# Earlier head products, earlier divisions and a separate bias matmul in an eight-layer transformer stack

## The reference

```python
# L2 attention
att = einsum('bhqd,bhkd->bhqk', q, k) / scale          # 512 x 512, 16 heads, causal
y = einsum('bhqk,bhkd->bhqd', softmax(att), v)
# L3 feed-forward, its head attention
h = _rmsnorm(x, gamma1)
q = (h @ Wq + bq).reshape(b, t, H, HD)
kv = ((h @ Wdown + bdown) @ Wup + bup).reshape(b, t, H, 2 * HD)
k, v = jnp.split(kv, 2, axis=-1)
att = jax.nn.softmax(einsum('bthd,btgd->bthg', q, k) / sqrt(HD), axis=-1)   # 16 x 16 per token
out = einsum('bthg,btgd->bthd', att, v)
```

## Time and profile before

| | |
|---|---|
| median of 3 runs | 6042.43 us (6034.11 to 6050.51) |
| profiled execution, its own time | 6034.11 us |
| its span | 6032.4 us, mean granted TensorE clock 0.875 of full |
| busy share | PE 78%, PEld 45%, DVE 61%, POOL 36%, ACT 31% |
| first maximum to last division of L2 attention, first pair | 134.3 us |
| DMA over the span | 24 GB/s |

### The profile page before, as it was taken

How to read it: one execution, slowest core, us unless ns; L and a number is a source line. 1 busy time by engine, 2 the same in 40 slices (tenths; PEclk the granted TensorE clock), 3 DMA queues, 4 the chain that set the end, 5 groups by cost and what they waited for, 6 DMA issues and landing times. The chain is left out here.

```text
span 6032.4 us, 97232 instructions
## 1 busy us (share of the span) xinstructions
PE 4713.6 (78%) x37160; PEld 2735.5 (45%) x37160; DVE 3697.0 (61%) x11081; ACT 1851.2 (31%) x2829; POOL 2161.3 (36%) x2704
## 2 busy tenths in 40 slices
PE   5979797979797979595877868778687786877772
PEld 3444445444444444363443544535435444354442
DVE  3646464646464646364768567686686766857765
ACT  2333343334333334242323224132331322412320
POOL 1323232323232222444525236153361443614525
PEclk9989898989898989797888888888888888888886
DMA  4000000000000000372000000000000000000000
GB/s 146 6 18 6 18 6 18 6 18 6 18 6 18 6 18 6 112 232 74 4 15 13 8 20 4 15 14 6 18 6 12 18 5 17 8 9 20 3 15 5
DMA packets 141914, 146.71 MB, mean 24 GB/s; under 512 B 31256, under 2 KB 126042, under 8 KB 141042
## 3 DMA queue, kind: packets, MB, share of 16 engines
q1 hardware_dynamic: 114274, 93.48, 5.3%
q0 software_dynamic: 18432, 37.79, 2.2%
q10 hardware_dynamic: 8736, 8.91, 0.5%
HBM read 69.64 MB, written 62.59 MB: 22 GB/s over the span
## 5 line engine op out<-in xcount | busy, mean ns | idle before, releaser
L792 DVE CUSTOM_DVE_ANT_0 twin<-twin,w_mask_row 128x512 f32<-128x512 f32 (+3 forms) x2048 | 951.0, 521 | 329.7 <-PE twin L1761 328.3
L1761 PE MATMUL twin<-arena 32*128 32x128 f32 (+3 forms) x4096 | 799.4, 517 | 39.6 <-DMA arena<-hres 16.8
L1779 PE MATMUL twin<-arena 32*128 32x128 f32 (+3 forms) x4096 | 784.2, 499 | 35.3 <-DVE arena L792 33.9
L1707 PE MATMUL twin<-w_ident_b 128*128 128x512 bf16 x1536 | 454.9, 450 | 383.7 <-DVE mv L752 157.9
L1435 ACT ACTIVATE arena<-twin 128x768 f32<-128x768 f32 (+1 forms) x544 | 479.3, 881 | 691.6 <-PE twin L1790 387.5
L1779 PEld LDWEIGHTS twin<-arena 32*128 32x128 f32 x4096 | 342.8, 195 | 471.7 <-issue 283.3
L695 POOL TENSOR_SCALAR ve<-mv 128x4 f32<-128x4 f32 x128 | 27.7, 216 | 1467.8 <-DVE mv L752 1467.2
L321 POOL DMA_INDIRECT got<-sorted_y,back x288 | 281.1, 976 | 539.6 <-ACT ring L1641 289.0
L1707 PEld LDWEIGHTS twin<-w_ident_b 128*128 128x128 bf16 x1536 | 157.7, 112 | 651.5 <-DVE mv L752 180.6
L313 POOL DMA_INDIRECT sorted_x<-got,w_mo_first_slots x288 | 282.4, 981 | 467.5 <-DVE ring L866 302.2
L1761 PEld LDWEIGHTS twin<-arena 32*128 32x128 f32 x4096 | 353.6, 204 | 196.8 <-issue 109.2
(11 more groups left out here) (440 smaller groups left out, 10008.1 us busy)
## 6 DMA issues: line engine op xcount, KB each, us to landing
sorted_y<-arena SPq DMA_DIRECT2D x96, 256.0 KB, 2.8
sorted_x<-zeros ACTq DMA_DIRECT2D x2, 4096.0 KB, 19.9
a<-sorted_x SPq DMA_DIRECT2D x64, 128.0 KB
b<-sorted_x SPq DMA_DIRECT2D x64, 128.0 KB, 2.5
hres<-sorted_x SPq DMA_DIRECT2D x64, 128.0 KB
sorted_x<-got,w_mo_first_slots POOLq DMA_INDIRECT x288
got<-sorted_y,back POOLq DMA_INDIRECT x288
x_out<-w_l_w SPq DMA_DIRECT2D x18, 256.0 KB, 2.3
```

Of the source, the lines that this page charges most:

```text
L792: last = dve.tensor_tensor_reduce(s[:, e, at:at + w], s[:, e, at:at + w], W["mask_row"][:, T - w:T], -1.0, 3e38, ALU.add, ALU.min, into)
L1707: pe.matmul(into, ident_b, ident_b.unsqueeze(1).broadcast_to([P, NT, P]), start=True, stop=True, skip_group_check=True)
L1761: last = pe.matmul(s[:, e, at:at + w], queries[r, P * i:P * (i + 1)], keys[r, 0:w], start=(at == 0), stop=True, skip_group_check=True)
L1779: last = pe.matmul(s[:, e, at:at + w], keys[r, P * m:P * (m + 1)], queries[r, P * m:T], start=(at == 0), stop=(tag == "l2"), skip_group_ch ...
```

## The change

It has four parts, all in the second loop.

- The products run two ahead: four of them stand before the first mask instead of two, and six quartets instead of seven carry two each. TAKE_STEP moves the reductions with them: the first four products are reduced from (-2, 3) to (0, 0), and the last two in quartet 6 instead of 7. `head_maxima`, `head_sums` and `head_outputs` on VectorE move from quartets 2, 3, 4, 5, 6 and 8 to 0, 1, 3, 4, 5 and 7, and `head_exponents` from (2, 3) and (5, 0) to (0, 3) and (4, 0).
- In every quartet of L2 attention `spread_sums` and `invert` move from step 3 to step 2, and `divide` from step 5 to step 3.
- The bias of the up-projection in `l3_front` is no longer a 65th row of ones in the down-projection's output. The down-projection gives 64 rows, the up-projection multiplies 64 rows, and a second matmul per token tile adds the bias: a row of ones, 1 x 128, by the bias, 1 x 256.
- The bias is a weight of its own, loaded once at the start.

```diff
@@ gpsimd, l2_masks and the layer loop @@
-                                        product(2 + 2 * c)
+                                        product(4 + 2 * c)
                                 if c < HEAD_QUARTETS:
-                                    product(3 + 2 * c)
+                                    product(5 + 2 * c)
...
-                                for m in range(2):
+                                for m in range(4):
                                     product(m)
                                 l2_masks()
@@ vector, twin_attention @@
-                                    if u == (2 if tag == "l1" else 5):
+                                    if u == (2 if tag == "l1" else 3):
                                         divide(c - 1)
@@ vector, l2_attention, beside @@
-                                if (c, u) == (2, 1):
+                                if (c, u) == (0, 1):
                                     head_maxima(0)
+                                if (c, u) == (1, 1):
+                                    head_sums(0)
                                 if (c, u) == (3, 1):
-                                    head_sums(0)
+                                    head_maxima(1)
                                 if (c, u) == (4, 1):
-                                    head_maxima(1)
+                                    head_sums(1)
                                 if (c, u) == (5, 1):
-                                    head_sums(1)
-                                if (c, u) == (6, 1):
                                     head_outputs(0)
-                                if (c, u) == (8, 1):
+                                if (c, u) == (7, 1):
                                     head_outputs(1)
@@ scalar, twin_attention and l2_attention @@
-                                    if tag == "l2" and u == 3:
+                                    if tag == "l2" and u == 2:
                                         invert(c - 1)
...
-                                if (c, u) == (2, 3):
+                                if (c, u) == (0, 3):
                                     head_exponents(0)
-                                if (c, u) == (5, 0):
+                                if (c, u) == (4, 0):
                                     head_exponents(1)
@@ tensor, twin_attention @@
-                                    elif u == 3:
+                                    elif u == 2:
                                         spread_sums(c - 1)
@@ tensor and scalar, l3_front @@
-                                pe.matmul(pb(q, 0)[0:65], W["l3f_wd"], F[q][:, PAD:], start=True,
+                                pe.matmul(pb(q, 0)[0:64], W["l3f_wd"], F[q][:, PAD:], start=True,
                                           stop=True).then_inc(sg["f_down_mm"], 1)
...
                                     o = pb3(q, 2 + t // 2, 2)[:, t % 2]
-                                    pe.matmul(o, ht_dt[q][0:65, t * P:(t + 1) * P], W["l3f_wup"], start=True, stop=True,
+                                    pe.matmul(o, ht_dt[q][0:64, t * P:(t + 1) * P], W["l3f_wup"], start=True, stop=False,
+                                              skip_group_check=True)
+                                    pe.matmul(o, W["ones"][0:1, :], W["l3f_bup"], start=False, stop=True,
                                               skip_group_check=True).then_inc(sg["f_kv_mm"], 1)
...
-                                act.activation(ht_dt[q][0:65], pb(q, 0)[0:65], ACT.Identity,
-                                               bias=W["l3f_bd"][0:65, 0:1]).then_inc(sg["f_dt"], 1)
+                                act.activation(ht_dt[q][0:64], pb(q, 0)[0:64], ACT.Identity,
+                                               bias=W["l3f_bd"][0:64, 0:1]).then_inc(sg["f_dt"], 1)
@@ tables @@
-HEAD_QUARTETS = 7
-TAKE_STEP = {(-1, 1): (0, 0), (-1, 2): (0, 1), (-1, 4): (1, 0), (0, 0): (1, 1)}
+HEAD_QUARTETS = 6
+TAKE_STEP = {(-2, 3): (0, 0), (-2, 4): (0, 1), (-1, 0): (1, 0), (-1, 1): (1, 1), (-1, 2): (2, 0), (-1, 3): (2, 1),
+             (-1, 5): (3, 0), (0, 0): (3, 1)}
...
-    TAKE_STEP[c_ + 1, 0], TAKE_STEP[c_ + 1, 2] = (2 + 2 * c_, 0), (2 + 2 * c_, 1)
+    TAKE_STEP[c_ + 1, 0], TAKE_STEP[c_ + 1, 2] = (4 + 2 * c_, 0), (4 + 2 * c_, 1)
@@ weights @@
+    a["l3f_wup"] = g["L3_ffn_Wup"].reshape(64, H, 2, DH).transpose(0, 2, 1, 3).reshape(64, 2 * D)
+    a["l3f_bup"] = g["L3_ffn_bup"].reshape(H, 2, DH).transpose(1, 0, 2).reshape(1, 2 * D)
```

More of the change, by code:

```diff
@@ L2373 @@
 BUSY = 6
-HEAD_QUARTETS = 7
-TAKE_STEP = {(-1, 1): (0, 0), (-1, 2): (0, 1), (-1, 4): (1, 0), (0, 0): (1, 1)}
+HEAD_QUARTETS = 6
+TAKE_STEP = {(-2, 3): (0, 0), (-2, 4): (0, 1), (-1, 0): (1, 0), (-1, 1): (1, 1), (-1, 2): (2, 0), (-1, 3): (2, 1),
+             (-1, 5): (3, 0), (0, 0): (3, 1)}
 for c_ in range(HEAD_QUARTETS):
-    TAKE_STEP[c_ + 1, 0], TAKE_STEP[c_ + 1, 2] = (2 + 2 * c_, 0), (2 + 2 * c_, 1)
-    TAKE_STEP[c_ + 1, 4], TAKE_STEP[c_ + 1, 5] = (3 + 2 * c_, 0), (3 + 2 * c_, 1)
+    TAKE_STEP[c_ + 1, 0], TAKE_STEP[c_ + 1, 2] = (4 + 2 * c_, 0), (4 + 2 * c_, 1)
+    TAKE_STEP[c_ + 1, 4], TAKE_STEP[c_ + 1, 5] = (5 + 2 * c_, 0), (5 + 2 * c_, 1)
 STATE_BANK = ((4, 5, 4), (6, 7, 5))
```

5 lines of the change are left out of this document (1 added, 4 removed).

## The result

The changed kernel takes 6239.39 us, the median of 4 runs (6223.85 to 6252.54), against 6038.95 (4 runs, 6034.11 to 6050.51): 1.0328 times as long, 95% interval 1.0302 to 1.0355. It is slower, as forecast, but by 200 us where the prediction had 74 to 79, and outside its range. The profiled execution took 6226.76 us, its span 6225.1 at a mean granted clock of 0.850 of full (before 0.875).

The account below looks back on a forecast made before the run. VectorE's list bounds L2 attention up to the shift of (5, 1); later TensorE waits for masks behind GpSimd's products. Attention +4.7 and bias +5.0 us, eight times, make 78, plus 0.5 once: 79, forecast 6116 us, range 6062 to 6150.

Parts of the forecast that it names:

- The bias matmul: End of the loop body: four more matmuls a sequence, 3.6 us, plus 1.4 for changes of shape, +5.0 us a body.
- Its bound of 8: Upper bound of the bias term: 8 us a body, at twice the passes' time.
- Spread sums a step earlier: L2 attention, quartets 1 to 5: about 0.5 us of new VectorE idle in each, +2.5 us a body.
- its bound of 5: Upper bound of the spread term: 5 us, if a half clock makes the spread take twice as long.
- The earlier division gives nothing back: L2 attention: dividing sooner gains nothing, since VectorE's total counts in that stretch, not its order.
- The subtraction: `head_maxima` at (0, 1): its subtraction meets a GpSimd product and takes the dearer earlier time, +1.1 us a body.
- `head_outputs`: The second head step moved to where a GpSimd product runs, at (5, 1): +0.5 us a body.
- The first rival: GpSimd's product holds the subtraction 2 us more, `head_outputs` 1 to 1.5: +3 us a body, 6140 us; chance 0.13.
- Reductions: VectorE up to the shift of (5, 1): more reductions +4.5, `head_outputs` +0.6, `head_sums` filling idle -1.5; sum +3.6 us.
- The tail: Quartets 6 and 7 lose their products, mask waits and half clock: 4.1 us gained, less spread delays, net -3 us.
- The rival of the low clock: Attention's third window has the low clock each time: +3.7 us a body, 30 in all, 6146 us; chance 0.07.

Follow-up runs that it names:

- e14: The changed kernel with VectorE's shift ahead of the head steps in step (c, 1); 1.0195 of before.
- e4: The kernel before with the bias part alone, its bias matmul having 64 rows (63 of zeros) instead of one; 1.0057 of before.
- e2: The kernel before with only spread_sums, invert and divide at their new steps; 1.0069 of before.
- e10: The kernel before with spread_sums, invert and divide at their new steps and VectorE's shift ahead of the head steps; 0.9983 of before.
- e13: The kernel before with one edit, VectorE's shift ahead of the head steps in step (c, 1); 0.9983 of before.
- e6: The kernel before with spread_sums and invert moved to step 2 and the division left at step 5; 1.0132 of before.
- e3: The kernel before with only the earlier products, reductions and head steps; 1.0040 of before.
- e8: The whole change without its bias part, the bias as in the kernel before; 1.0155 of before.
- e1: The kernel before with the bias part of the change alone; 1.0158 of before.
- e9: The kernel before with the bias part alone, its bias matmul having 32 rows (31 of zeros) instead of one; 1.0187 of before.
- e7: The kernel before with the bias part alone, two one-row matmuls of 512 columns placed ahead of the four of 64 rows; 1.0152 of before.

## Why the prediction was wrong

The direction and the bound of the front were right. The sum per body was 9.7 us and is 26.3. Two steps failed: the bias matmul, which cost 95 us instead of 40, and the earlier spread sums, which with the other steps cost 42 us alone and some 80 in the whole (e14) instead of 28. By the prediction's own steps:

- **The bias matmul (+5.0, the larger of the two).** The columns' 3.6 were right (e4: 3.5 a body). The change of shape was taken as 0.1 us from the earlier trace rows and is 0.19, 2.7 a body instead of 1.4. What is left of the 11.9, 5.7, is the clock, which the sum put at nothing: the earlier trace rows gave no reason to expect it, and no row before showed shapes alternating pass by pass. Its bound of 8 was too low for the same reason. Why the clock falls stays open.
- **Spread sums a step earlier (+2.5, the other).** Alone the steps cost 7.9 us of attention (e2). The prediction followed quartet 3 and named the wait for the shift, but priced only what comes after the spread, at full clock; half clock was its bound of 5, not its term. TensorE already stood 1.50 us in front of that spread, with `head_sums` ahead of the shift, and moved a step ahead it stands 2.9 us there in the mean, and 2.8 to 3.5 in quartets 2 to 6 (e2). What carries the loss is what stands ahead of the shift on VectorE, with TensorE's wait of up to 4.2 us and the half clock behind it: e10 and e13. In quartet 6 that is an instruction which is itself held by a product.
- **"The earlier division gives nothing back"** was wrong as well: without it (e6) the moved spread costs nearly twice as much in the ratio, 1.6 us more in attention.
- **The subtraction (+1.1) and `head_outputs` (+0.5).** The first rival was the truer: 3.84 us, +2.6, in all bodies, and `head_outputs` at (5, 1) takes 2.5 us in the mean instead of 0.69, +1.8. The Trainium skill (SBUF — State Buffer, "SBUF: two separate sides"), as told beside this step, has VectorE held until GpSimd's instruction ends, and the times here agree: both end about 1.1 and 0.55 us after the product.
- **Reductions (+3.6).** The first two windows are as forecast but for the subtraction, 31.3 us. The 1.5 taken off for `head_sums`, which was to fill the third window's idle time, was not there: VectorE idles 2.7 to 3.7 us in that window in e3, at a granted clock of 0.77 to 0.82 where before has 0.99 or 1.00 in seven of eight bodies. The products alone lose 10.6 us up to the shift of (5, 1) in e3's profile.
- **The tail (-3.0).** The products alone gain 5.1 us there (e3), and no matmul of quartet 7 waits for a mask as in the earlier trace rows; in the whole change 2.8 are left. The steps alone cost 3.4 there (e2), where the prediction had 1.
- **The whole.** 13.1 us of attention are near e2's 7.9 and e3's 5.4. The ratios show more than the parts (e8), and what the shift in front takes off the whole (e14) exceeds what it takes off the steps (e10) by about that much. Which wait makes it isn't shown. The steps at (1, 1), (3, 1), (4, 1) and (5, 1) delay shifts for which TensorE now stands still; `head_maxima` at (0, 1) doesn't, as no spread follows it in that quartet.

The rival of the low clock was right for the third window, 14.5 us in the mean against 11.3. But the half clock that came on top lies mostly elsewhere: taking the clock's loss times the length, it is 2.7 us a body in the third window, 5.6 in the sixth to eighth, and 9 between the last division and the next body. No rival had the clock at the bias, or TensorE standing still for a shift.

## What to carry to other kernels

Before an instruction that waits is moved ahead of work that doesn't, look at what stands in front of its releaser on the other engine, in the worst round of the loop and not in a typical one. A stall of TensorE is paid twice, as the wait and as the clock after it. An addition folded into a matmul as one more row is cheap; as matmuls of another shape between the first ones, in a stretch that nothing hides, it cost about three times its columns (0.0158 against 0.0057). And where two engines' instructions can hold each other, a shift of half a microsecond decides which one waits, so a reorder has to be looked at in every round for such a meeting.

## What the runs showed of the hardware

- A VectorE subtraction of two SBUF tiles that started while a GpSimd product ran ended 1.07 to 1.09 us after the product in most cases: 3.84 us (after, e3), 3.24 (e14) and 2.30 to 2.32 (the second one of the changed kernel) instead of 1.22. In some bodies it ended that long after the two masks behind the product instead. Two masks that followed a held subtraction took 1.76 us for both instead of 0.8.
- Which of the two starts first decides: a VectorE product of 128x512 that began 0.02 us ahead of GpSimd's took its 0.69 us, and GpSimd's took 5.96; one that began 0.97 us behind took 5.01, and GpSimd's 5.43.
- VectorE's reductions of one SBUF tile were not held: 1.20 to 1.24 us in every run, also beside a product, as the one at 3240.62 ahead of the held subtraction.
- A matmul of 256 columns starts 0.43 us after the last at full clock (e4), and 0.625 where the next one has another number of rows (64 against 1 or 32; after, e1, e9).
- The granted clock fell in the middle of uninterrupted matmuls when they were 64 rows alternating with 1 or 32 (e1, e9), or 1 row first (e7), in all eight bodies of each, and never in sixteen passes of 64 rows (e4).
